# Where the small weights of a two-layer block are loaded and prepared

## The reference

```
q, k   = bf16(x @ Wq.T), bf16(x @ Wk.T)         # then rotary embedding
s[i]   = sum over j <= i of exp(q[i].k[j] / sqrt(128))
attn   = relu(s * fc1_w + fc1_b) @ fc2_w.T + fc2_b     # 1 -> 16 -> 128
ffn    = relu(x @ W1[1] + b1[1]) @ W2[1] + b2[1]       # 128 -> 256 -> 128
```

## Time and profile before

| what | value |
|---|---|
| median of 3 runs | 91.88 us (91.78 to 91.89) |
| the profiled execution | 91.72 us |
| its span, first to last instruction | 90.0 us |
| PE busy (matmuls) | 82.5 us, 92% |
| DVE busy | 76.6 us, 85% |
| ACT busy | 71.0 us, 79% |
| POOL busy | 56.8 us, 63% |
| granted clock of TensorE | 0.997 of full speed |
| share of the chain that ended last | PE 67%, ACT 20%, DMA 4%, POOL 2% |

### The profile page before, as it was taken

How to read it: one execution, slowest core, us unless ns; L and a number is a source line. 1 busy time by engine, 2 the same in 40 slices (tenths; PEclk the granted TensorE clock), 3 DMA queues, 4 the chain that set the end, 5 groups by cost and what they waited for, 6 DMA issues and landing times.

```text
span 90.0 us, 1535 instructions
## 1 busy us (share of the span) xinstructions
PE 82.5 (92%) x444; PEld 49.5 (55%) x444; DVE 76.6 (85%) x202; ACT 71.0 (79%) x210; POOL 56.8 (63%) x83
## 2 busy tenths in 40 slices
...
DMA packets 11900, 7.64 MB, mean 85 GB/s; under 512 B 867, under 2 KB 10996, under 8 KB 11892
## 3 DMA queue, kind: packets, MB, share of 16 engines
...
...
## 4 chain that ended last, share of the span: by engine, by line
PE 67%; ACT 20%; DMA 4%; POOL 2%; SPq 2%; issue 1%; POOLq 1%; DVE 0%
PE psum L735 24%; ACT psum L569 15%; PE psum L810 15%; PE psum L761 12%; PE psum L727 7%; DMA wqk_f<-wqk_t 4%; PE psum L789 3%; POOL rstd L505 2%; SPq L331 2%; PE psum L781 1%; ACT qk L521 1%; PE psum L710 1%; PE psum L765 1%; PE psum L772 1%; PE psum L800 1%
## 5 line engine op out<-in xcount | busy, mean ns | idle before, releaser
L505 POOL TENSOR_TENSOR rstd<-ve,half_neg 128x4 f32<-128x4 f32 (+2 forms) x38 | 34.8, 925 | 13.8 <-DVE ve L357 9.6
L569 ACT ACTIVATE psum<-psum 128x1024 f32<-128x1024 f32 (+7 forms) x48 | 36.7, 764 | 1.4 <-PE psum L761 0.6
L761 PE MATMUL psum<-qk_r 128*128 128x512 bf16 (+3 forms) x80 | 20.7, 349 | 1.4 <-ACT psum L569 0.6
L810 PEld LDWEIGHTS psum<-w_c,hid 128*128 128x128 f32 x128 | 15.6, 192 | 1.3 <-DVE cols_n L521 0.4
L735 PE MATMUL psum<-cols_n,wqk 128*128 128x512 f32 (+1 forms) x36 | 16.1, 556 | 0.0
L810 PE MATMUL psum<-w_c,hid 128*128 128x128 f32 x128 | 16.1, 278 | 0.0
L735 PE MATMUL psum<-cols_n,w_c 128*128 128x512 f32 (+1 forms) x36 | 15.6, 552 | 0.0
L761 PEld LDWEIGHTS psum<-qk_r 128*128 128x128 bf16 x80 | 6.6, 97 | 12.9 <-ACT psum L569 6.4
L727 PE MATMUL psum<-ident,rows_n 128*128 128x128 f32 x64 | 10.2, 277 | 0.1
L357 POOL TENSOR_SCALAR ve<-stats 128x4 f32<-128x4 f32 (+2 forms) x9 | 2.1, 233 | 11.6 <-DVE stats L642 6.6
L727 PEld LDWEIGHTS psum<-ident,rows_n 128*128 128x128 f32 x64 | 7.2, 141 | 3.8 <-issue 1.6
...
## 6 DMA issues: line engine op xcount, KB each, us to landing
...
qk_swap<-qk SPq DMA_DIRECT2D x14, 128.0 KB, 2.3
...
x_s<-x SPq DMA_DIRECT2D x2, 128.0 KB, 3.1
w_f<-w SPq DMA_DIRECT2D x2, 128.0 KB, 3.2
table<-tables SPq DMA_DIRECT2D x2, 128.0 KB, 4.3
...
```

What stands on the lines that cost most here:

```text
L505: ready[k].done(eng.tensor_tensor(rstd[:, g, STAT_SLOT[k], t], ve[:, g, STAT_SLOT[k], t], half_neg[:, 0:tiles], ALU.pow), n)
L569: exps.done(eng.activation(area, area, ACT.Exp, scale=scale_qk, accum_out=sums[:, g, s, j:j + 1]), n, j, s)
L761: mm = eng.matmul(psum[:, own[0] + i, 0:width], query, qk_r[:, g0 + c, 1, 0:width], start=True, stop=c < gb)
L810: mm = eng.matmul(bank[:, j * P:(j + 1) * P], hid[:, g, h, (j0 + j) * P:(j0 + j + 1) * P], w2_c[:, h, :], start=not seeded and h == 0, sto ...
```

## The change

Nothing of the arithmetic's meaning is changed. In the order, load_fc, the fifth load so far (behind wqk), goes behind load_x.8 and is the ninth; the steps fc.0, fcmean.0, +fc.0 and fcspread.0 go from the front's first units to behind k.1 (fc.0, now in bank 6 and ahead of k.4), behind +k.4.A (fcmean, +fc, ahead of +q.4.A), and behind rstd1.7 (fcspread). w2mean goes from ACT (four instructions) to DVE as one bn_stats over both halves, interleaved, and from behind k.3 to between rope.0 and rope.4. w2 goes from ACT (two instructions) to POOL as one tensor_tensor with a broadcast mean, behind norm1.7.P. b2mean and b2 stay on ACT and go from ahead of +k.1.A to behind exp.2.0.0. All other steps keep their order.

```diff
-load_x.3 blank.9#7 blank.1.256#7 load_x.0 repeat.0 load_x.4 mask.0 load_wqk.0 load_fc.0 stat1.3 load_x.1 stat1.0
-eps1.3.P load_x.6 eps1.0.D stat1.4 rstd1.0 wqk.0#0 load_x.2 rstd1.3 eps1.4.A norm1.0.D load_x.8 tr1.0#1 fc.0#2
-+wqk.0.A rstd1.4 load_w2.0 stat1.1 +tr1.0.A norm1.3.D eps1.1.A load_x.5 fcmean.0 k.0#1 rstd1.1 norm1.4.D tr1.3#0
-load_x.7 +fc.0 q.0#3 norm1.1.D +tr1.3.A load_table.1 fcspread.0 stat1.6 tr1.4#2 tr1.1#4 load_table.4 stat1.2 +tr1.4.A
-q.3#0 load_b1.0 +tr1.1.A stat1.8 +k.0.A k.3#2 w2mean.0 load_table.0 eps1.6.D stat1.5 rstd1.6 +q.3.A k.1#1 load_table.2
-load_b2.0 stat1.7 eps1.8.A k.4#4 +k.3.A rstd1.8 norm1.6.D +q.0.A swap.3 q.4#0 eps1.2.A +k.4.A rstd1.2 norm1.8.D
-tr1.6#3 +q.4.A load_table.3 cos.3.D rot.0#4 tr1.8#2 +tr1.6.A swap.4 norm1.2.D q.1#0 +tr1.8.A q.6#3 cos.4.D eps1.5.A
-w2.0 b2mean.0 b2.0 sin.3.D tr1.2#2 +k.1.A rstd1.5 k.6#5 rope.3.D +q.6.A +tr1.2.A cos.0.D scores.2.2.0#3 eps1.7.A
-sin.0.D scores.2.3.0#1 exp.2.2.0 k.8#2 rstd1.7 sin.4.D exp.2.3.0 scores.2.0.0#3 rope.0.D scores.2.1.0#4 +k.6.A q.8#6
-rope.4.D exp.2.1.0 swap.6 norm1.5.D +k.8.A k.2#5 exp.2.0.0 cos.6.D +q.8.A scores.3.2.0#12 sum.2.D +q.1.A
+load_x.3 blank.9#7 blank.1.256#7 load_x.0 repeat.0 load_x.4 mask.0 load_wqk.0 stat1.3 load_x.1 stat1.0 eps1.3.P
+load_x.6 eps1.0.D stat1.4 rstd1.0 wqk.0#0 load_x.2 rstd1.3 eps1.4.A norm1.0.D load_x.8 load_fc.0 tr1.0#1 +wqk.0.A
+rstd1.4 load_w2.0 stat1.1 +tr1.0.A norm1.3.D eps1.1.A load_x.5 k.0#1 rstd1.1 norm1.4.D tr1.3#0 load_x.7 q.0#3
+norm1.1.D +tr1.3.A load_table.1 stat1.6 tr1.4#2 tr1.1#4 load_table.4 stat1.2 +tr1.4.A q.3#0 load_b1.0 +tr1.1.A stat1.8
++k.0.A k.3#2 load_table.0 eps1.6.D stat1.5 rstd1.6 +q.3.A k.1#1 fc.0#6 load_table.2 load_b2.0 stat1.7 eps1.8.A k.4#4
++k.3.A rstd1.8 norm1.6.D +q.0.A swap.3 q.4#0 eps1.2.A +k.4.A fcmean.0 +fc.0 rstd1.2 norm1.8.D tr1.6#3 +q.4.A
+load_table.3 cos.3.D rot.0#4 tr1.8#2 +tr1.6.A swap.4 norm1.2.D q.1#0 +tr1.8.A q.6#3 cos.4.D eps1.5.A sin.3.D tr1.2#2
++k.1.A rstd1.5 k.6#5 rope.3.D +q.6.A +tr1.2.A cos.0.D scores.2.2.0#3 eps1.7.A sin.0.D scores.2.3.0#1 exp.2.2.0 k.8#2
+rstd1.7 fcspread.0 sin.4.D exp.2.3.0 scores.2.0.0#3 rope.0.D w2mean.0.D scores.2.1.0#4 +k.6.A q.8#6 rope.4.D exp.2.1.0
+swap.6 norm1.5.D +k.8.A k.2#5 exp.2.0.0 b2mean.0 b2.0 cos.6.D +q.8.A scores.3.2.0#12 sum.2.D +q.1.A scores.0.1.0#3
+cos.8.D swap.8 scores.3.3.0#67 exp.0.1.0 cos.1.P +k.2.D rot.1#0 exp.3.2.0 tr1.5#4 sin.1.D q.2#3 exp.3.3.0 +tr1.5.D
...
@@ -204,6 +204,7 @@
         b2_s = sb("b2_s", [P, P], BF16)
         ones_b = sb("ones_b", [P, P], BF16)
         means = sb("means", [P, 4], F32)
+        w2_stats = sb("w2_stats", [P, HC, 3], F32)
         spare = sb("spare", [P, 4, P], F32)
 
         x_s = sb("x_s", [P, n_groups, TILES, P], F32)
@@ -244,7 +245,7 @@
         exps, summed, biased = signal("exp", "act"), signal("sum", "dve"), signal("bias", "dve")
         x1_done, out_done = signal("x1", "dve"), signal("out", "dve")
         x1_scaled, out_scaled = signal("xs", "dve"), signal("ys", "dve")
-        mean_fc, mean_w2, w2_done = signal("fcmean", "act"), signal("w2mean", "act"), signal("w2", "act")
+        mean_fc, mean_w2, w2_done = signal("fcmean", "act"), signal("w2mean", "dve"), signal("w2", "pool")
         mean_b2, b2_done = signal("b2mean", "act"), signal("b2", "act")
         fc_spread = signal("fcspread", "pool")
         b2_split, b2_rows = signal("b2split", "pool"), signal("b2rows", "dve")
@@ -495,6 +496,11 @@
                     make_mask()
                 elif name == "fcspread":
                     spread_fc()
+                elif name == "w2":
+                    mean_w2.wait(eng, 0)
+                    w2_done.done(eng.tensor_tensor(w2_c[:, :, :], w2_f[:, :, :],
+                                                   w2_stats[:, :, 1].unsqueeze(2).to_broadcast([P, HC, P]),
+                                                   ALU.subtract), 0)
                 elif name == "repeat":
                     make_repeat()
                 elif name[0:4] == "rstd":
@@ -578,17 +584,6 @@
                     mean_fc.wait(eng, 0)
                     taken["fc"].done(eng.activation(fc2_c[:, :], bank_of("fc", 0)[:, P:2 * P], ACT.Identity,
                                                     bias=means[:, 2:3]), 0)
-                elif name == "w2mean":
-                    eng.wait_ge(l_w2, 16)
-                    for h in range(HC):
-                        ins = eng.activation(spare[:, h, :], w2_f[:, h, :], ACT.Copy, scale=-1.0 / P,
-                                             accum_out=means[:, h:h + 1])
-                    mean_w2.done(ins, 0)
-                elif name == "w2":
-                    mean_w2.wait(eng, 0)
-                    for h in range(HC):
-                        ins = eng.activation(w2_c[:, h, :], w2_f[:, h, :], ACT.Identity, bias=means[:, h:h + 1])
-                    w2_done.done(ins, 0)
                 elif name == "b2mean":
                     eng.wait_ge(l_b2, 16)
                     mean_b2.done(eng.activation(spare[:, 3, :], b2_f[:, :], ACT.Copy, scale=-1.0 / P,
@@ -676,6 +671,10 @@
                                                        rstd[:, g, STAT_SLOT[k], j0 + j:j0 + j + 1],
                                                        prev[:, g, j0 + j, :], ALU.mult, ALU.add)
                     (x1_done if k == 3 else out_done).done(ins, n)
+                elif name == "w2mean":
+                    eng.wait_ge(l_w2, 16)
+                    mean_w2.done(eng.bn_stats(w2_stats[:, :, :].rearrange("p h c -> p (h c)"),
+                                              w2_f[:, :, :].rearrange("p h o -> p o h")), 0)
                 elif name == "b2rows":
                     b2_split.wait(eng, 0)
                     eng.wait_ge(s_zero_b2, 1)
```

More of the change, by code:

```diff
@@ L38 @@
 STEPS = """
[L39 to L58, removed]
@@ L59 @@
-eps4.3.P exp.4.0.0 +h0.2.D rstd4.3 h1.2#2 eps4.0.D sum.1.D exp.4.3.0 scores.8.2.1#01 +h1.2.D norm4.3.P scores.4.0.1#4
+load_x.3 blank.9#7 blank.1.256#7 load_x.0 repeat.0 load_x.4 mask.0 load_wqk.0 stat1.3 load_x.1 stat1.0 eps1.3.P
+load_x.6 eps1.0.D stat1.4 rstd1.0 wqk.0#0 load_x.2 rstd1.3 eps1.4.A norm1.0.D load_x.8 load_fc.0 tr1.0#1 +wqk.0.A
+rstd1.4 load_w2.0 stat1.1 +tr1.0.A norm1.3.D eps1.1.A load_x.5 k.0#1 rstd1.1 norm1.4.D tr1.3#0 load_x.7 q.0#3
+norm1.1.D +tr1.3.A load_table.1 stat1.6 tr1.4#2 tr1.1#4 load_table.4 stat1.2 +tr1.4.A q.3#0 load_b1.0 +tr1.1.A stat1.8
@@ new lines @@
+swap.6 norm1.5.D +k.8.A k.2#5 exp.2.0.0 b2mean.0 b2.0 cos.6.D +q.8.A scores.3.2.0#12 sum.2.D +q.1.A scores.0.1.0#3
+cos.8.D swap.8 scores.3.3.0#67 exp.0.1.0 cos.1.P +k.2.D rot.1#0 exp.3.2.0 tr1.5#4 sin.1.D q.2#3 exp.3.3.0 +tr1.5.D
+norm1.7.P w2.0.P hT.2#0 scores.3.1.0#12 +q.2.D scores.3.0.0#45 +hT.2 sin.6.D q.5#6 exp.3.1.0 swap.2 rope.1.D
+scores.0.0.0#0 exp.3.0.0 rope.6.D scores.0.3.0#1 load_w1.0 fc2.2#23 exp.0.0.0 sin.8.D exp.0.3.0 scores.5.0.0#45
+cos.2.D +q.5.A scores.5.3.0#01 rope.8.D exp.5.0.0 k.5#7 stat3.2.D scores.0.2.0#6 exp.5.3.0 sin.2.D scores.7.1.0#45
```

7 lines of the change are left out of this document (added).

## The result

The changed kernel took 94.19 us, median of 21 runs (92.55 to 94.78), against 91.80 us for the kernel before (21 runs, 91.12 to 93.08). The ratio is 1.0122 [1.0096, 1.0148]: slower. The ratio leaves out, for either kernel, executions that took over 1.5% longer than its fastest. Of the 21 of the changed kernel, 14 took 93.38 to 94.78 and 7 took 92.55 to 92.79. So there are two things to explain: about 1 us that every execution loses, and some 1.5 us more that two thirds of them lose. The forecast of 92.2 had the sign and not the size; its range ended at 92.75, and only five of the 21 lie within it.

The account below looks back on a forecast made before the run. The end was taken to follow ACT's backlog at 22.5 us, unless PE or DVE fed it later. DVE's +0.65, less 0.25 of room and 0.1 of gaps, gave +0.3: 91.72+0.3 = 92.02, 92.2 on the median's scale, range 91.45 to 92.75.

Parts of the forecast that it names:

- Step 1: At the front, load_fc's later place and fcspread's removal let PE's dense run start 0.45 us earlier (10.2 to 9.75).
- Step 2: The fc matmuls inside PE's dense run, ahead of k.4, take 0.55 us, so k.4 is made at +0.1 us.
- Step 3: ACT moves by -0.73 us up to exp.2.0.0, stands at 0.00 behind b2; its exponentials would start 0.18 us earlier.
- Step 4: swap.4's DMAs wait 0.6 us longer for q.4's evacuation but land at 18.6; sin.4 on DVE moves by -0.5 us.
- Step 5: w2mean on DVE, ahead of rope.4, takes 0.35 us and does not wait.
- Step 6: fcspread's selects on POOL, beside DVE's two-input instructions, cost 0.9 us; DVE is at +0.65 at 22.2 us.
- Step 7: DVE's lateness reaches ACT through hT.2, less 0.25 us of room: +0.4, after small later gaps +0.3.
- Step 8: w2 on POOL, 0.61 us, begins at 25.05 beside DVE's PSUM evacuations, at no cost when DVE is 0.65 late.

Follow-up runs that it names:

- before_warm: The kernel before with 13 instead of 9 blank matmuls of 512 columns: 91.89 us, ratio 1.0013 to the kernel before.
- fc_only: The kernel before with only the fc part of the change (load, matmuls, means and centring, fcspread moved), 9 blanks: 92.59 us, ratio 1.0092.
- w2b2_warm: The kernel before with only the w2 and b2 part of the change, and 13 blank matmuls instead of 9: 92.11 us, ratio 1.0066.
- after_warm: The changed kernel with 13 instead of 9 blank matmuls of 512 columns: 92.90 us, ratio 1.0132 to the kernel before.
- after_fcpe_early: The changed kernel with 13 blanks, load_fc and the fc matmuls back at their old places, means, centring and fcspread still late: 92.54 us, ratio 1.011.
- after_spread: The changed kernel with 13 blanks and fcspread moved on POOL from behind rstd1.7 to behind rstd1.5: 92.66 us, ratio 1.0131.
- after_b2late: The changed kernel with 13 blanks, b2mean and b2 moved to about 54 us on ACT, b2split and b2rows behind them: 93.33 us, ratio 1.0184.
- after_w2late: The changed kernel with 13 blanks, w2mean on DVE and w2 on POOL moved to about 48 to 50 us: 92.59 us, ratio 1.0085.
- w2b2_only: The kernel before with only the w2 and b2 part of the change, 9 blanks: 93.18 us, ratio 1.0129.

## Why the prediction was wrong

The direction was right; the 0.3 us were about 1.0, and the low clock level had no place in it. The shorter executions took 92.55 to 92.79, at the upper edge of the range, but a hit there would have been luck: the terms behind the 0.3 were others. Distances between moments of one execution, in us, all read at the starts:

| from ... to | before | before_warm | fc_only | w2b2_warm | after_warm |
|---|---|---|---|---|---|
| PE's run (q.3) to k.4's evacuation | 3.21 | 3.21 | 4.04 | 3.21 | 4.04 |
| on to exp.2.2.0 | 5.47 | 5.48 | 5.58 | 5.05 | 5.02 |
| on to exp.0.1.0 | 3.80 | 3.80 | 3.79 | 4.19 | 4.19 |
| on to exp.5.0.0 | 5.55 | 5.56 | 5.56 | 6.01 | 6.01 |
| on to the end of the span | 61.9 | 61.9 | 61.9 | 61.9 | 61.9 |

**Step 1 failed.** "Both reasons give PE's dense run [...] a start 0.45 us earlier (10.2 to 9.75)." Its run began at 10.07 before, at 10.02 in after_warm and 9.88 in fc_only: 0.05 to 0.19 gained. What the step said of DVE came true in the main: norm1.3 started at 7.05 instead of 7.62, and norm1.1 shrank to 0.43 us. But PE had no time to give. It was busy without a break from k.0's start to the run's, here in the kernel before:

```profile
7.78:10.07 2.29, 2.29 (x16) 1.77 (x15) 2.29 (x5) 1.69 (x7) 2.05 (x4) 1.00 0.97 275
```

In before_warm and after_spread these matmuls took 2.06 us, so 0.23 could be won between the two at most, and k.0 did not come earlier (7.82). norm1.1 also began late, at 9.26 instead of 8.88, since it now waits 0.58 us for rstd1.1, whose pow on POOL took 1.20 us instead of 0.74.

**Step 2 is the failed step that weighs most.** "k.4 is made at -0.45+0.55 = +0.1 us": it was +0.78, and +0.64 in fc_only. Two errors add up. The gain of step 1 was missing, and the 0.55 was 0.83: the run q.3 to q.4 ended at 10.07+4.03 = 14.10 us before and at 12.90+1.98 = 14.88 in after_warm, from a start 0.05 earlier. Of these 0.83, 0.64 pass between the starts of the first fc matmul (12.26) and of k.4 (12.90), as long as the four took where they stood before, so that the dense stream saved nothing of it; the other 0.19 pass just ahead of them and in k.4's first matmul. Where they had stood, the fc matmuls cost nothing: PE waits there for tr1.0's evacuation anyway, and that wait is the gap of 0.47 us in after_warm. By after_fcpe_early the place of these matmuls is worth 0.41 us at exp.5.0.0.

**Step 3 failed as well.** "Up to exp.2.0.0 ACT moves by [...] -0.73 us": exp.2.2.0 was at +0.33. Of the 1.06 us between the two, 0.68 is step 2's. Most of the rest is work that was taken off ACT and came back as idle time, 1.07 us ahead of k.4's evacuation, 0.27 ahead of q.6's and 0.24 ahead of exp.2.2.0, all behind PE. w2b2_warm shows it without fc: 1.9 us of work removed, 0.43 of time won. The prediction itself had said that w2mean "stands where PE is the bound, so it is worth nothing by itself"; that held for two thirds of w2 and b2 too (0.43 won of 1.32), and the sum counted them in full. Behind the first exponentials b2's 0.73 cost 0.39 (3.80 to 4.19): the evacuations of q.8 and q.1 with the wait behind them took 1.07 us before (21.48 to 22.55) and 0.74 behind b2 (22.53 to 23.27). So "0.00 behind b2" became +0.72.

**Step 4** was half right: sin.4 did not wait for its DMA, at 18.90 instead of 19.13, -0.23 where -0.5 was said. **Step 5** was right: w2mean took 0.42 us, and it was covered.

**Step 6 was right in size and wrong in weight.** 0.44 on norm1.5 and 0.43 on cos.6 make 0.87 us, against the 0.9 taken; the selects themselves took 0.94 and 0.97 instead of 0.64 and 0.70, so each engine held up the other. The Trainium skill's SBUF — State Buffer, section "Who interferes with whom", names this pair, calls the ports that the two share an exclusive lock, and says, at DVE's two-port modes, that the second to issue "fully blocks". The trace agrees, for two-input instructions too. rope.4, the first select, norm1.5, the second select and cos.6 began in this order, each inside the one before, and ended at 20.85, 21.35, 21.90, 22.39 and 22.93: the engines took turns, about 0.5 us each, and each instruction is longer by what was left of the other engine's. But after_spread takes half of it away and wins nothing, since q.8's evacuation behind b2 set cos.8.

**Step 7** has its second half shown, in another kernel: after_b2late has the chain from cos.8 over sin.1 and hT.2 to ACT, with cos.1 on POOL as about half of DVE's delay. In the change itself h1T shows no gap for PE; ACT was late by its own b2 and the front. The forecast's +0.3 came out of this path, which set nothing.

**Step 8 failed.** "beside PSUM evacuations of DVE when DVE is 0.65 late (no cost)": DVE was late by more (cos.8 at 23.20 instead of 22.18) and w2 still met sin.6, as POOL's own instructions ahead of it moved along, to 26.00. It cost sin.6 0.28 us, and 0.31 us at the end (after_w2late). A meeting was worked out with one engine moved and the other left in place.

In sum, up to exp.5.0.0 after_warm is 1.23 us longer than the kernel before: +0.83 for the fc matmuls, -0.45 ahead of exp.2.2.0 for the work taken off ACT, +0.39 for b2 among the exponentials, and +0.46 behind, of which after_w2late takes 0.28 away (w2 beside sin.6); the other 0.18 were not traced. The parts nearly add: fc_only has +0.93 and w2b2_warm +0.42. In the times they are 0.9% and 0.7%, together 1.3%, with intervals too wide to tell. That b2's removal would give its 0.39 back was not shown, since after_b2late (3.84 in that row) opened another chain. The rival that the gaps of ACT swallow the gain, so that b2 and the fc matmuls stand alone, was missing from the list; it needed no number that the trace of before didn't show.

The part beyond 1.0 us: the change opens PE's idle time ahead of k.0 (0.47 us), and two thirds of the executions are long; both that were profiled had PE at 1.2 GHz at the front. That the blanks prevent it is shown (none of 61 executions came near 94). That the gap left by fc is what makes it frequent is argued: w2b2_only, which keeps fc in place, had a profile with it as well, and the kernel before had long executions too (5 of its 21 took 92.86 to 93.08).
